# One VectorE pass over two PSUM banks for two neighbouring result blocks, in a fused group-norm and channel-attention kernel

## The reference

```python
qkv = xt @ w_qkv                       # xt: group norm of x, tokens x 192 channels
q, k, v = jnp.split(qkv, 3, axis=-1)   # then 8 heads of 24 channels
q = q / jnp.maximum(jnp.sqrt(jnp.sum(q * q, axis=-2, keepdims=True)), EPS)
k = k / jnp.maximum(jnp.sqrt(jnp.sum(k * k, axis=-1, keepdims=True)), EPS)
attn = jax.nn.softmax(jnp.einsum('bhpn,bhnq->bhpq', k * temperature, q), axis=-1)
out = jnp.einsum('bhnp,bhpq->bhnq', v, attn)   # back to tokens x 192
out = out @ w_out + b_out
x = x + out
```

## Time and profile before

| | us |
|---|---|
| median of 3 runs | 446.87 (445.19 to 448.86) |
| the profiled execution | 446.14 |
| its span | 444.4 |
| busy PE / DVE / ACT / POOL | 359.3 / 320.2 / 258.2 / 161.8 |

### The profile page before, as it was taken

One profiled execution on the slowest core, in us unless ns is written; L12 is line 12 of the kernel. 1 busy time (PEld: TensorE's weight loads), 2 busy tenths in 40 slices (PEclk: granted clock), 3 DMA queues, 4 the chain that ended last, 5 costly groups with the idle time before them and its releaser, 6 DMA issues.

```text
span 444.4 us, 9461 instructions
## 1 busy us (share of the span) xinstructions
PE 359.3 (81%) x3772; PEld 240.2 (54%) x3772; DVE 320.2 (72%) x762; ACT 258.2 (58%) x392; POOL 161.8 (36%) x116
## 2 busy tenths in 40 slices
PE   0134784889988999899889998899989988999686
PEld 0023644675557646675557565665667556755342
DVE  4789921897769983998579857997499848356564
ACT  1072648782698449971988188835996298711100
POOL 0066327710592029402761067203940285103000
PEclk9996975699989998999989998999899999999699
DMA  8999300001696058803891189406960463025266
GB/s 287 265 278 274 71 2 0 1 1 73 191 301 187 1 184 283 281 1 125 272 324 29 71 258 299 121 27 185 310 227 1 143 200 88 1 95 179 89 189 197
DMA packets 30684, 67.92 MB, mean 153 GB/s; under 512 B 5360, under 2 KB 11824, under 8 KB 30640
## 3 DMA queue, kind: packets, MB, share of 16 engines
q1 hardware_dynamic: 30352, 66.86, 48.6%
q10 hardware_dynamic: 288, 0.46, 0.3%
HBM read 29.55 MB, written 28.31 MB: 130 GB/s over the span
## 4 chain that ended last, share of the span: by engine, by line
PE 51%; DVE 26%; ACT 9%; issue 5%; POOL 3%; DMA 2%; SPq 1%; ACTq 0%; DVEq 0%; POOLq 0%
PE u_ps L901 26%; PE s_ps L901 10%; PE g_ps L901 8%; ACT tok L510 3%; DVE dq L741 3%; POOL l_sb L428 3%; DVE bnst L670 2%; ACT h_sb L492 2%; DMA x_sb<-in_x_dram 2%; PE u_ps L947 2%; DVE xn L699 2%; ACT mh L537 2%; DVE pf L817 2%; DVE rk L743 2%; DVE x_sb L825 2%
## 5 line engine op out<-in xcount | busy, mean ns | idle before, releaser
L428 POOL TENSOR_TENSOR l_sb<-xn,h_sb 128x768 f16<-128x768 f32 x72 | 120.9, 1698 | 52.7 <-ACT h_sb L492 46.0
L901 PE MATMUL g_ps<-tok 128*128 128x64 f16 (+1 forms) x864 | 88.8, 242 | 26.3 <-ACT tok L510 13.2
L825 DVE SCALAR_TENSOR_TENSOR x_sb<-u_ps,bias,x_sb 128x384 f32<-128x384 f32 x144 | 82.2, 610 | 18.4 <-PE u_ps L901 18.2
L510 ACT COPY tok<-u_ps 128x768 f16<-128x768 f16 x104 | 78.5, 804 | 20.7 <-PE u_ps L950 20.4
L901 PEld LDWEIGHTS g_ps<-tok 128*128 128x128 f16 x864 | 57.9, 100 | 55.1 <-DVE tok L729 17.1
L901 PE MATMUL u_ps<-h_sb,ml 128*128 128x384 f16 (+1 forms) x336 | 78.7, 343 | 7.6 <-DVE x_sb L825 7.6
L492 ACT ACTIVATE h_sb<-x_sb,rb 128x768 f16<-128x768 f32 x72 | 72.7, 1019 | 20.7 <-DVE rb L722 20.7
L670 DVE BATCH_NORM_STATS2 bnst<-x_sb 128x6 f32<-128x512 f32 (+1 forms) x120 | 68.0, 623 | 7.6 <-DMA x_sb<-in_x_dram 7.5
L486 ACT ACTIVATE xn<-x_sb,rb 128x768 f32<-128x768 f32 x63 | 63.4, 1017 | 9.5 <-DVE rb L722 7.7
L947 PE MATMUL u_ps<-id,h_sb 128*128 128x128 f16 x288 | 51.5, 232 | 13.1 <-POOL l_sb L428 12.7
L434 POOL TENSOR_TENSOR grs<-gvar,minus_half 128x3 f32<-128x3 f32 x8 | 6.8, 852 | 136.0 <-DVE gvar L713 136.0
(11 more groups left out here) (145 smaller groups left out, 627.9 us busy)
## 6 DMA issues: line engine op xcount, KB each, us to landing
x_sb<-in_x_dram SPq DMA_DIRECT2D x48, 384.0 KB, 5.6
out_dram<-x_sb SPq DMA_DIRECT2D x48, 384.0 KB, 2.9
x_sb<-in_x_dram SPq DMA_DIRECT2D x48, 192.0 KB, 5.7
out_dram<-x_sb SPq DMA_DIRECT2D x48, 192.0 KB, 2.8
hl<-h_sb SPq DMA_DIRECT2D x48, 96.0 KB, 2.6
hl<-l_sb SPq DMA_DIRECT2D x48, 96.0 KB, 2.6
h_sb<-in_groups_dram ACTq DMA_DIRECT2D x1, 384.0 KB, 4.5
w<-in_L_conv_w_qkv_dram SPq DMA_DIRECT2D x1, 288.0 KB
```

Of the source, the lines that this page charges most:

```text
L428: nc.gpsimd.tensor_tensor(l_sb[:, par, t, cols], xn[:, c % XN_RING, :], h_sb[:, par, t, cols], ALU.subtract).then_inc(l_ok, 1)
L510: nc.scalar.copy(tok[:, j % TOK_RING, :, :].rearrange("p b n -> p (b n)"), slot_ps(j)).then_inc(tok_a, 1)
L825: V.scalar_tensor_tensor(out=xs, in0=block_ps(n), scalar=bias[:, t:t + 1], in1=xs, op0=ALU.add, op1=ALU.add).then_inc(out_ok, 1)
L901: return nc.tensor.matmul(dst, lhs, rhs, start=start, stop=stop, skip_group_check=True)
```

## The change

DVE ends two neighbouring blocks with one instruction of 768 columns, which reads 384 columns from each of two neighbouring banks of `u_ps`. `result` is called only after odd n, for blocks n - 1 and n; it waits until PE has finished both, and adds 2 to `out_ok` when it is done. What the other engines do and wait for is as before. On DVE, what the tables hang behind an even block now stands ahead of the pass that ends this block.

```diff
+        def blocks_ps(n):
+
+            return u_ps[:, (SLOTS + n) % RING:(SLOTS + n) % RING + 2, 0:BW]
...
             def result(q, n):
-                (t, c), w = OUTS[n], BW
-
-                dve.wait_ge(out_mm, q * NO + n + 1)
-                xs = xcol(q, t, c, w)
-                V.scalar_tensor_tensor(out=xs, in0=block_ps(n), scalar=bias[:, t:t + 1], in1=xs,
-                                       op0=ALU.add, op1=ALU.add).then_inc(out_ok, 1)
+                t, c = OUTS[n]
+
+                dve.wait_ge(out_mm, q * NO + n + 2)
+                xs = xcol(q, t, c, 2 * BW).rearrange("p (k w) -> p k w", k=2)
+                V.scalar_tensor_tensor(out=xs, in0=blocks_ps(n), scalar=bias[:, t:t + 1], in1=xs,
+                                       op0=ALU.add, op1=ALU.add).then_inc(out_ok, 2)
...
                 for n in range(NO):
-                    if small:
-                        result(p, n)
+                    if small and n % 2:
+                        result(p, n - 1)
```

## The result

| | before | changed |
|---|---|---|
| median, us | 446.19 (445.19 to 448.86, 4 runs) | 467.82 (464.88 to 470.76, 4 runs) |
| profiled execution, its span | 446.14, 444.4 | 467.20, 465.1 |
| ratio to before | | 1.0475, 95% interval 1.0392 to 1.0558 |

The account below looks back on a forecast made before the run. PE bounds the kernel, waiting for single passes that come late, not for DVE's throughput. 446.14 plus 18.4 + 1.4 + 0.4 - 1.7 = +18.5 gave 464.6 us; two clock falls, +3.2, made about 468; range 460 to 476.

Parts of the forecast that it names:

- The rival by which 9 us of spared DVE time count: DVE's time decides in stage A, reached 9 us sooner over the kernel: faster, 437 us; chance 0.03.
- The price of a pass: On DVE, a pass of 768 columns takes 1.01 us, 0.925 from one to the next; bounds 0.81 and 1.14.
- The plain rhythm: Where no small DVE steps stand ahead, PE has slack over two blocks (1.63 us), so wide passes cost nothing.
- Stalls A, B and C: In stage B of pairs 0 to 5, blocks 4, 10 and 16 start +1.21, +3.21 and +3.07 us later; 18.4 in all.
- The advance of 0.32 at the Gram step: Without block 0's pass ahead, DVE's second Gram part and all behind it run 0.32 us earlier.
- Stage A: Between stages B, PE's waits for `tok` give none of the shift back, except after pair 3.
- The exception behind pair 3: In stage A there, `dq` took 3.02 us against 1.14 behind pair 1; 1.7 us expected back.
- The rival of a shift given back in all pairs: Stage A's waits for `tok` shrink, six times 1.7 us less: 454.4 us; chance 0.12.
- Pair 6: Wide passes there delay block 4 by 1.11 us and block 12 by 1.42 in all; +1.4 in the sum.
- The clock: New idle time at block 10 lets PE's clock fall 0 to 6 times, 0 to 9.6 us; two taken, +3.2.
- The price of a fall: Each fall of PE's clock, judged from blocks 16 and 17 and the transposes behind, loses an estimated 1.6 us.
- What would show it: Signs listed: block starts in pairs 0 to 5, PE's waits for the line about 47 us, DVE busy about 311.

Follow-up runs that it names:

- the last single form: The kernel before (a pass per block) with DVE's small steps moved, POOL's `norms` behind chunk 5 and ACT's chunk 6 later: 437.41 us, ratio 0.9788.
- the wide form: The changed kernel, all passes wide, with DVE's small steps moved in pairs 0 to 5: 446.55 us, ratio 1.0004 to the kernel before.

## Why the prediction was right

**What bounds.** That PE waits for single late passes and not for DVE's throughput holds: six wide passes in places with nothing ahead moved the time by 0.3%, and one in a place behind `t2` by 2.2%. The rival by which 9 us of spared DVE time count was wrong in every form; DVE's busy time fell by 19.6 us and the kernel became slower.

**The price of a pass.** 1.017 us measured, 1.01 taken from the slope of another form. From one to the next it is 1.94 - 1.02 = 0.92, as taken. The plain rhythm costs nothing, as forecast: in pair 7, which has no small steps, block 16 starts at 13.92 in both kernels. That the pass reads two banks costs nothing that can be seen.

**Stalls A, B and C.** All three came in the places and sizes given, to 0.02 us, in all of pairs 0 to 5, but for block 16 of pair 5, ahead of which the clock fell. The advance of 0.32 at the Gram step came too: its second part starts 2.21 after block 0 instead of 2.56, and the passes at 4.28 instead of 4.61.

**Stage A.** That it gives nothing back holds. PE reaches the third `tok` earlier (3.8 to 4.2 after the first transposes against 4.6 to 5.2) because `dq` no longer waits for POOL, and then waits for ACT's `tok` of slot 4 at 6.2 to 6.6, where it was 6.2 to 6.7. The exception behind pair 3 came as well: 6.45 instead of 8.11, that is -1.66 where I had -1.7. Over the pair only 1.17 of it is left (50.48 - 48.58 = 1.90 instead of 3.07), because more of the stretch from block 16 to the transposes ran at the lower clock (3.2 us instead of 2.7). The rival of a shift given back in all pairs counts the 1.7 behind pair 3 twice; with five pairs it would be 456.1 and not 454.4, still far off.

**Pair 6** was under-sized, +2.2 instead of +1.4. The term missed one user of `t2`: PE's `scores` stand behind block 9 there, and `t2` now stands behind a pass that takes 0.4 longer.

```profile
421.07 0.29 PE L905 MATMUL s_ps<-tq,wh 128*96 128x96 f16 x2 [0.33 <-DVE tq L822]
```

So block 10 starts at 16.23, 1.50 later than before and not 1.10. The other 0.4 is at block 17, part of which ran at the lower clock.

**The clock** was put at two falls, +3.2 us. The idle time ahead of block 10 is 1.82 us and not 2.1, since 164.62 in that sum is the end of block 10 in the kernel before; block 9 ends at 163.69 + 1.21 = 164.90. In the profiled execution one of six idle stretches at block 10 brought a fall (pair 5, whose block 12 came 0.6 later than in the others and block 16 1.98), and behind pair 2 the fall that every pair had before didn't come. The granted clock of four stretches of the changed kernel, ahead of block 10 and behind block 16 of pair 1, behind pair 2, and behind block 10 of pair 5:

```profile
166.00:169.00 3.00, 2.57 (x17) 1.34 (x15) 2.97 (x7) 1.48 (x4) 1.78 (x2) 1.00 0.75 202
180.80:183.80 3.00, 3.00 (x21) 1.73 (x20) 0.81 (x1) 0.91 (x2) 2.59 (x2) 0.50 0.93 353
230.00:233.00 3.00, 2.73 (x30) 1.50 (x29) 1.61 (x2) 2.05 (x3) 3.00 (x3) 1.00 1.01 293
372.00:375.00 3.00, 3.00 (x15) 1.24 (x12) 1.02 (x1) 3.00 (x4) 3.00 (x3) 0.50 0.37 144
```

Pair 5 took 2.3 us more than the three stalls by this, and pair 2 took 1.2 less. With smaller shifts of where the fall came in the other pairs the clock's term is about 0.8 us here and not 3.2. The price of a fall, 1.6 us by estimate, is 1.58 in the kernel with one wide pass, up to block 14. Pair 7, taken as evidence against falls, was a poor witness: it begins behind the same 2.2 us of idle time in all eleven traces, and in three of them (with six wide passes, with one, and in the last single form) the clock is low there and block 4 starts at 4.71 to 4.88 instead of 3.26. So the forecast of 468 is right to 0.2 us of the median partly by luck: the sum without falls was 464.6, pair 6 was 0.8 too low, the clock 2.4 too high in this execution, 0.6 came ahead of pair 0 and 0.3 outside the span. The other runs, up to 470.8, have no profile.

**What would show it.** Two numbers of that list were off. The waits for the line came to 61.6 us and not 47: the view counts a stall for PE and again for its weight loads, and I had added the stall to the total once. And DVE's busy time fell to 300.6, not to 311. The passes account for 10.9 of the 19.6 us (busy 82.2 before, 71.3 now), and `dq` and `rk` for 12.7 (21.8 and 9.2), since they no longer waited for POOL; the other instructions took 3.5 more. The two behind pair 1:

```profile
184.43 0.55 DVE L745 TENSOR_TENSOR dq<-r,id 96x384 f32<-96x384 f32 x1
184.89 0.15 DVE L747 TENSOR_TENSOR rk<-r,temp 96x4 f32<-96x4 f32 x1
```

The first took 1.14 there before. A busy time can hold a wait.

## What to carry to other kernels

Before merging two instructions that give buffers back, write down for each buffer what will stand ahead of its release, and who asks for it first; the saved fixed cost counts only if that engine is the one that is waited for. Where a merge moves releases behind other work, moving that work is worth more than the merge: it took back all 21 us here, and the same move with single passes and a gap for one starved step was 2.1% faster than the kernel before. When a gain in one stage doesn't arrive, look in the next stage for a step that now meets a neighbour it used to miss.

## What the runs showed of the hardware

A DVE `tensor_tensor` with single-precision operands in SBUF (`dq`, 0.55 us alone) doesn't share with POOL's `tensor_tensor`: it ended 0.40 us behind the POOL work that was running, and where two POOL instructions came back to back it waited for both, 3.59 us in all. In the same kernels the passes of 384 and 768 columns, one operand of which is in PSUM, kept 0.62 and 1.02 us at most, beside POOL or not.

The clock did not fall in a fixed way: behind the same 1.82 us of idle time at block 10 it fell in three pairs of six in one kernel, in two in another and in one in the changed kernel; behind 1.42 us (two passes at the wide one's place) in none. What a fall costs depends on who sets the pace. Where PE did, it was 1.58 us up to block 14. With moved steps it fell in stage A behind pairs 1 and 2 of the wide form, 30.3 and 30.9 us after block 0, and these two pairs took 47.19 and 47.20 us, as the others did. Falls that cost some 1.6 us each are of the size of the spread between runs; that they are the spread's cause was not tested.
